# Two attentions whose maxima, sums and output fold leave float32 on TensorE

## The reference

```
x = x + cross_attention0(ctx, layernorm(x))   # 8 heads of 128, keys and values from [norm(x), norm(ctx)]: 2113 rows
x = x + experts0(layernorm(x))                # top 2 of 8 experts
x = x + cross_attention1(ctx, layernorm(x))   # 8 heads of 32, keys and values from ctx: 1601 rows
x = x + experts1(layernorm(x))                # top 2 of 8 experts
# each attention: softmax(q k^T * scale) v, per head; attention 0 has an output projection Wo
```

## Time and profile before

| | us |
|---|---|
| runs, median of 3 | 2718.49 (2716.02 to 2721.48) |
| the profiled execution | 2723.15 |
| its span, first to last instruction | 2721.6 |
| TensorE busy in the span | 2477.8 (91%) |
| DVE, ACT, POOL busy | 1865.4, 1675.5, 1636.6 |

### The profile page before, as it was taken

How to read it: one execution, slowest core, us unless ns; L and a number is a source line. 1 busy time by engine, 2 the same in 40 slices (tenths; PEclk the granted TensorE clock), 3 DMA queues, 4 the chain that set the end, 5 groups by cost and what they waited for, 6 DMA issues and landing times. The chain is left out here.

```text
span 2721.6 us, 46305 instructions
## 1 busy us (share of the span) xinstructions
PE 2477.8 (91%) x15187; PEld 1489.6 (55%) x15314; DVE 1865.4 (69%) x3467; ACT 1675.5 (62%) x2694; POOL 1636.6 (60%) x1442
## 2 busy tenths in 40 slices
PE   4999999999999999999999389867999999869997
PEld 2455555555555555555554268734555554447886
DVE  5678767787777786777676565347787888677443
ACT  3465665556655566555555375436787878758664
POOL 3467766677667676656567244416676769825443
PEclk9999999999999999999999589979999999969999
DMA  3000000000000000000000383231111101076223
GB/s 117 25 1 1 4 22 1 1 1 1 25 1 1 1 1 1 1 1 1 1 1 0 112 243 78 41 101 40 32 41 26 48 19 30 3 215 188 46 46 66
DMA packets 88377, 107.92 MB, mean 40 GB/s; under 512 B 16322, under 2 KB 77715, under 8 KB 88163
## 3 DMA queue, kind: packets, MB, share of 16 engines
q1 hardware_dynamic: 67140, 76.37, 9.3%
q0 software_dynamic: 19200, 24.97, 5.7%
q10 hardware_dynamic: 1856, 4.19, 0.4%
HBM read 68.75 MB, written 25.88 MB: 35 GB/s over the span
## 5 line engine op out<-in xcount | busy, mean ns | idle before, releaser
L396 POOL TENSOR_TENSOR a_acc<-a_acc,a_pf 128x512 f32<-128x512 f32 (+1 forms) x480 | 645.3, 1344 | 388.0 <-ACT a_pf L524 367.8
L1993 POOL TENSOR_TENSOR c_pl<-c_pf,c_ph 128x512 f16<-128x512 f32 x320 | 378.3, 1210 | 169.0 <-ACT c_ph L2092 168.7
L524 ACT ACTIVATE a_pf<-a_psS 128x1024 f32<-128x1024 f32 (+1 forms) x288 | 281.2, 976 | 303.8 <-PE a_psS L663 300.2
L813 DVE TENSOR_TENSOR a_pl<-a_pf,a_ph 128x512 f16<-128x512 f32 x448 | 405.4, 914 | 28.2 <-ACT a_ph L530 28.2
L789 DVE TENSOR_REDUCE a_mx<-a_psA 128x1 f32<-128x512 f32 x512 | 344.9, 685 | 48.8 <-PE a_psA L600 42.6
L530 ACT ACTIVATE a_ph<-a_psS 128x1024 f16<-128x1024 f32 (+1 forms) x288 | 281.0, 976 | 0.0
L1303 POOL DMA_INDIRECT f_sums<-f_xn,f_sidx x78 | 138.9, 1781 | 228.1 <-DVE f_xn L1668 191.6
L2324 DVE TENSOR_REDUCE c_mx<-c_psA 128x1 f32<-128x512 f32 x384 | 251.0, 685 | 34.4 <-PE c_psA L2163 32.4
L2085 ACT ACTIVATE c_pf<-c_psS 128x1024 f32<-128x1024 f32 x192 | 197.7, 1030 | 89.4 <-PE c_psS L2197 88.5
L784 DVE TENSOR_TENSOR a_vl<-a_psA,a_vh 128x256 f16<-128x256 f32 (+1 forms) x272 | 115.2, 423 | 167.2 <-ACT a_vh L469 164.3
L1162 DVE TENSOR_TENSOR f_xn<-f_xn 128x256 f16<-128x256 f32 x312 | 129.6, 424 | 127.8 <-ACT f_xn L1133 123.5
(11 more groups left out here) (329 smaller groups left out, 6382.8 us busy)
## 6 DMA issues: line engine op xcount, KB each, us to landing
f_stage<-in_L_ffn_w SPq DMA_DIRECT2D x16, 1024.0 KB, 5.6
f_stage<-in_L_ffn_W SPq DMA_DIRECT2D x16, 1024.0 KB, 5.3
c_kst<-c_khs SPq DMA_DIRECT2D x64, 100.1 KB, 2.2
a_cx<-in_ctx SPq DMA_DIRECT2D x4, 1536.0 KB
c_cx<-in_ctx SPq DMA_DIRECT2D x12, 512.0 KB, 4.1
f_xrow<-f_xn SPq DMA_DIRECT2D x8, 512.0 KB, 3.2
f_sums<-X SPq DMA_DIRECT2D x2, 2048.0 KB, 12.4
c_kst<-c_kls SPq DMA_DIRECT2D x32, 100.1 KB, 2.2
```

The source lines that it names most:

```text
L396: g.tensor_tensor(acc[0:k, p, :], acc[0:k, p, :], pf[0:k, q % RF, i, :], ALU.add).then_inc(s_acc, 1)
L524: act.activation(pf[0:r, q % RF, 0:k, :], psS[q % 2][0:r, 0:k, :], ACT.Exp, scale=SCALE).then_inc(s_pF, 1)
L813: v.tensor_tensor(pl[0:r, q % RP, i, :], pf[0:r, q % RF, i, :], ph[0:r, q % RP, i, :], ALU.subtract).then_inc(s_pL, 1)
L1993: g.tensor_tensor(pl[0:r, q % RP, i, :], pf[0:r, q % RF, i, :], ph[0:r, q % RP, i, :], ALU.subtract).then_inc(s_pG, 1)
```

## The change

In both attentions three operations of TensorE on float32 operands are replaced.

- Attention 0, maxima: X and ACT's copy go. POOL multiplies a diagonal of -1 (`minus`, bfloat16) with the maxima, broadcast, so that `mrow` holds each maximum negated on a diagonal; the unchanged fourth matmul with ones adds up the column. POOL does it in unit 7 behind its additions, and TensorE waits for it at the fourth matmul of the next head's first tile.
- Attention 0, sums: ACT makes a float16 high half of `acc` at the beginning of unit 1 of the next head, POOL the low half at the beginning of unit 2, and S takes both against a float16 column. To fit float16, the exponentials are lifted by a factor of 16 through a bias column, and the column of fours becomes 4/16, the output's scale 1/(64 x 16).
- Attention 1, maxima: `mc` and the identity are float16, X is a plain matmul.
- Attention 1, output: after `out_copy`, ACT makes the high half at the end of unit 4 and DVE the low half at the beginning of unit 5; both lie in the buffer of `pw`, whose next write now waits for F. F moves from unit 4 to unit 5, place 2, with twice the matmuls, in float16.

```diff
@@ attention0, head_items
-                               (6, 3, ("L", m)), (7, 2, ("X", m))):
+                               (6, 3, ("L", m))):
@@ gpsimd
+            def sum_lo(n):
+                g.wait_ge(s_sh, n + 1)
+                if n >= 1:
+                    g.wait_ge(s_it, IDX[("S", n - 1)] + 1)
+                g.tensor_tensor(sl[:, :], acc[:, n % 2, :], sh[:, :], ALU.subtract).then_inc(s_sl, 1)
+
+            def row(n):
+                g.wait_ge(s_mc, n + 1)
+                g.tensor_tensor(mrow[:, n % 2, :].rearrange("p (t q) -> p t q", q=P),
+                                minus[:, :].unsqueeze(1).broadcast_to([P, ST, P]),
+                                mc[:, n % 2, :].unsqueeze(2).broadcast_to([P, ST, P]), ALU.mult).then_inc(s_mrow, 1)
...
+            row(0)
...
+                    if n >= 1 and u == SUM_AT:
+                        sum_lo(n - 1)
                     sums(n, u)
+                    if u == TOP and n + 1 < NH:
+                        row(n + 1)
@@ scalar
-                elif what[0] == "X":
-                    act.wait_ge(s_it, i + 1)
-                    act.activation(mrow[0:1, what[1] % 2, :], ps[0:1, :], ACT.Copy, scale=-1.0).then_inc(s_ah, 1)
+            def sum_hi(n):
+                act.wait_ge(s_acc, added(uid(n, U - 1)))
+                if n >= 1:
+                    act.wait_ge(s_it, IDX[("S", n - 1)] + 1)
+                act.activation(sh[:, :], acc[:, n % 2, :], ACT.Copy).then_inc(s_sh, 1)
...
+                    if n >= 1 and u == SUM_AT - 1:
+                        sum_hi(n - 1)
...
                     act.activation(pf[0:r, q % RF, 0:k, :], psS[q % 2][0:r, 0:k, :], ACT.Exp,
-                                   scale=SCALE).then_inc(s_pF, 1)
+                                   bias=lift[0:r, 0:1], scale=SCALE).then_inc(s_pF, 1)
@@ tensor
-                    pe.wait_ge(s_acc, added(uid(n, U - 1)))
+                    pe.wait_ge(s_sl, n + 1)
                     for it in range(ST):
-                        ins = pe.matmul(ps[:, it:it + 1], acc[:, n % 2, it * P:(it + 1) * P], four[:, :], start=True,
-                                        stop=True)
+                        for part in (sh, sl):
+                            ins = pe.matmul(ps[:, it:it + 1], part[:, it * P:(it + 1) * P], quarter[:, :],
+                                            start=part is sh, stop=part is sl)
...
-                        pe.wait_ge(s_ah, after_act(("X", n)))
                 triple(ps, kh[:, p, js], kl[:, p, js], qh[:, p, :], ql[:, p, :], True, False)
+                if u == 0 and i == 0:
+                    pe.wait_ge(s_mrow, n + 1)
                 ins = pe.matmul(ps, oneb[:, 0:r], mrow[:, p, :], start=False, stop=True)
@@ attention1, head_items
-            at[LAG][2].append(("F", n - 1))
+            at[LAG + 1][2].append(("F", n - 1))
@@ scalar
+            def out_hi(n):
+                act.wait_ge(s_oF, n + 1)
+                if n >= 1:
+                    act.wait_ge(s_it, IDX[("F", n - 1)] + 1)
+                act.activation(ofh[:, :], of[:, :], ACT.Copy, scale=1.0 / 64).then_inc(s_oH, 1)
...
                     if u == WHOLE:
                         if n >= 1:
-                            act.wait_ge(s_pv, uid(n - 1, WHOLE) + 1)
+                            act.wait_ge(s_it, IDX[("F", n - 1)] + 1)
...
                     for what in places[2] + places[3]:
                         item(what)
+                    if n >= 1 and u == LAG:
+                        out_hi(n - 1)
@@ tensor
-                        ins = pe.transpose(ps[0:1, it * P:(it + 1) * P], mc[:, n % 2, it:it + 1], identf[:, :])
+                        ins = pe.matmul(ps[0:1, it * P:(it + 1) * P], mc[:, n % 2, it:it + 1], ident[:, :], start=True,
+                                        stop=True)
...
-                    pe.wait_ge(s_oF, n + 1)
+                    pe.wait_ge(s_oL, n + 1)
                     for it in range(ST):
-                        ins = pe.matmul(ps[:, it * (DH + 1):(it + 1) * (DH + 1)], of[:, it * P:(it + 1) * P],
-                                        fold[:, :], start=True, stop=True)
+                        for part in (ofh, ofl):
+                            ins = pe.matmul(ps[:, it * (DH + 1):(it + 1) * (DH + 1)], part[:, it * P:(it + 1) * P],
+                                            fold[:, :], start=part is ofh, stop=part is ofl)
@@ vector
+            def out_lo(n):
+                v.wait_ge(s_oH, n + 1)
+                v.scalar_tensor_tensor(ofl[:, :], of[:, :], 1.0 / 64, ofh[:, :], ALU.mult, ALU.subtract).then_inc(s_oL, 1)
...
+                    if n >= 1 and u == LAG + 1:
+                        out_lo(n - 1)
```

More of the change, by code:

```diff
@@ L12 @@
 import itertools
+import math
 from contextlib import ExitStack
@@ L150, in opening @@
         out.insert(out.index(("M", 0, 0, 0)), ("B", 0))
-        return out + [("L", 0), ("B", 1), ("V", 0, v), ("X", 0)]
+        return out + [("L", 0), ("B", 1), ("V", 0, v)]
     OPEN = opening()
@@ L261, in attention0 @@
         oneb = sb("oneb", [P, P], BF16)
+        minus = sb("minus", [P, P], BF16)
         onef = sb("onef", [P, P], F32)
-        four = sb("four", [P, 1], F32)
+        quarter = sb("quarter", [P, 1], F16)
+        lift = sb("lift", [P, 1], F32)
         zcol = sb("zcol", [P, 1], F32)
@@ L299, in attention0 @@
         s_mc = sem("mc")
+        s_mrow = sem("mrow")
         s_sP = sem("sP")
@@ L343, in _ @@
         def _(g):
-            for t, v in ((mhalf, -0.5), (onef, 1.0), (four, 4.0), (mv, 0.0), (oneb, 1.0), (mrow, 0.0), (zcol, 0.0)):
+            for t, v in ((mhalf, -0.5), (onef, 1.0), (quarter, 4.0 / LIFT), (lift, math.log(LIFT)), (mv, 0.0), (oneb, 1.0), (zcol, 0.0)):
                 g.memset(t[:], v).then_inc(s_const, 1)
-            g.wait_ge(s_const, 7)
+            g.tensor_scalar(minus[:, :], identf[:, :], -1.0, None, ALU.mult).then_inc(s_const, 1)
+            g.wait_ge(s_const, 8)
             pools = [0]
@@ L425, in _ @@
                             item(what)
+            sum_lo(NH - 1)
             for what in CLOSE:
@@ L501, in out_hi @@
                     act.wait_ge(s_it, IDX[("O", n - 1, 1)] + 1)
-                act.activation(oh[:, :], psO[:, :], ACT.Copy, scale=1.0 / 64).then_inc(s_oH, 1)
+                act.activation(oh[:, :], psO[:, :], ACT.Copy, scale=1.0 / (64 * LIFT)).then_inc(s_oH, 1)
             for what in OPEN:
@@ L530, in _ @@
                     act.activation(ph[0:r, q % RP, 0:k, :], psS[q % 2][0:r, 0:k, :], ACT.Exp,
-                                   scale=SCALE).then_inc(s_pH, 1)
+                                   bias=lift[0:r, 0:1], scale=SCALE).then_inc(s_pH, 1)
                     for what in places[2] + places[3]:
                         item(what)
+            sum_hi(NH - 1)
             out_hi(NH - 1)
@@ L610, in item @@
                     n = what[1]
-                    pe.wait_ge(s_acc, added(uid(n, U - 1)))
+                    pe.wait_ge(s_sl, n + 1)
                     for it in range(ST):
-                        ins = pe.matmul(ps[:, it:it + 1], acc[:, n % 2, it * P:(it + 1) * P], four[:, :], start=True,
-                                        stop=True)
-                elif what[0] == "X":
-                    n = what[1]
-                    pe.wait_ge(s_mc, n + 1)
-                    for it in range(ST):
-                        ins = pe.transpose(ps[0:1, it * P:(it + 1) * P], mc[:, n % 2, it:it + 1], identf[:, :])
+                        for part in (sh, sl):
+                            ins = pe.matmul(ps[:, it:it + 1], part[:, it * P:(it + 1) * P], quarter[:, :],
+                                            start=part is sh, stop=part is sl)
                 elif what == ("B", 0):
@@ L1911, in attention1 @@
         s_oF = sem("oF")
+        s_oH = sem("oH")
+        s_oL = sem("oL")
         s_rl = sem("rl")
@@ L1973, in rstds @@
                 g.tensor_scalar(ve[:, :], mv[:, :, 1], EPS, None, ALU.add).then_inc(s_pool, 1)
-                g.wait_ge(s_pool, b + 1 if b == 0 else 2 + b + 1)
+                g.wait_ge(s_pool, b + 1 if b == 0 else 3 + b + 1)
                 g.tensor_tensor(rstd[:, :], ve[:, :], mhalf[:, :], ALU.pow).then_inc(s_rstd, 1)
@@ L2095, in _ @@
                         item(what)
+                    if n >= 1 and u == LAG:
+                        out_hi(n - 1)
+            out_hi(NH - 1)
         @block.tensor
@@ L2381, in _ @@
             out_copy(NH - 1)
+            out_lo(NH - 1)
             for what in CLOSE:
```

31 lines of the change are left out of this document (19 added, 12 removed).

## The result

The changed kernel takes 2775.19 us (median of 4 runs, 2769.04 to 2777.64) against 2718.37 for the kernel before on the same chip: ratio 1.0202, interval 1.019 to 1.0214. It is slower by 2%, where I forecast no change, and lies above my range of 2696 to 2738. The profiled execution took 2773.67 us with a span of 2772.1, against 2723.15 and 2721.6.

A forecast was written before the change was run, and what follows sets the result against it. TensorE bounds attention 0 (99% busy); in attention 1 three other engines run close to the head's time. Attention 0's +13.1 and attention 1's -14.1 give -1.0 on 2723.15, less 4.66 for the median: 2717 us, range 2696 to 2738.

The forecast's parts named there:

- X removed: Attention 0: turning the maxima leaves TensorE, 0.43 us in each of 31 heads, -13.3 us.
- S in float16, and the lift: Attention 0: float16 sums save 0.57 us in each of 32 heads, -18.2; the exponentials' bias column costs +2.2.
- the row, late: Attention 0 head ends: TensorE waits for POOL's row behind unit 7's additions, +42.5 us, between 34 and 52.
- start and end: Attention 0: -0.5 us at the start, +0.4 at the end for the sums' halves.
- The rest has cover: Attention 0: the sums' halves on ACT (0.6 us) and POOL (1.15) cost nothing, POOL being idle 14.5 us a head.
- r: Duration of POOL's row instruction at attention 0's head ends: taken as 1.4 us, between 1.1 and 1.75.
- case 4: Attention 0: DVE's low half has the port first, the row takes 1.75 us at 28 boundaries, +8.8: 2727 us; chance 23%.
- Heads without preparation: Attention 1, 14 heads: DVE's chain replaces TensorE's 0.78 us saving, 0.2 kept each, -2.8; bounds -10.9 and +2.8.
- Case 5: Attention 1: `out_lo` meets POOL and takes 1.2 us instead of 0.7, +12 us: 2730; chance 16%.
- Heads with preparation: Attention 1, 18 heads: new chain covered, 0.78 us saved each, -14.0, of which 2 goes to small waits: -12.0.
- X in float16: Attention 1: four float16 matmuls turn the maxima in 0.22 us instead of 0.43, 0.21 saved a head.
- my signs for a wrong forecast: Row waits under 30 or over 55 us; row outside 1.0-1.8; sums not half a microsecond shorter; late attention-1 heads outside 13.3-14.1.

The follow-up runs named there:

- run 4: Kernel before, with only attention 0's sums in float16 halves and the lifted exponentials; maxima's row and attention 1 as before: 2717.39 us, ratio 0.9974.
- run 3: Changed kernel with POOL's row of maxima in unit 7 moved ahead of its two additions: 2722.20 us, ratio 1.0 against the kernel before.
- Run 2: Attention 1 as changed, attention 0 as in the kernel before: 2739.82 us, ratio 1.0068.
- Run 10: Attention 0 as before; attention 1 makes both output halves but leaves them unused, F staying float32 at its old place: 2748.98 us.
- run 6: Kernel before, with only attention 1's maxima and identity in float16 and four float16 matmuls for X: 2724.27 us, ratio 0.9999.
- run 7: Only attention 1 changed; in 14 heads without preparation `out_lo` reads one operand from PSUM, the output's low half left out: 2734.32 us, ratio 1.0038.
- run 8: Only attention 1 changed, with DVE making both output halves straight from PSUM and ACT's step gone: 2733.04 us, ratio 1.0035.

## Why the prediction was wrong

Attention 0, by the steps of the sum (measured: differences of the stage between before, run 4, run 3 and after, which add up to +35.6):

| step | predicted | measured |
|---|---|---|
| X removed | -13.3 | -13.8 |
| S in float16, and the lift | -18.2 + 2.2 | -6.3 |
| the row, late | +42.5 | +55.7 |
| start and end | -0.1 | within the above |
| attention 0 | +13.1 | +35.6 |

- **X: right**, to 0.01 us in 26 of 31 heads.
- **S: the saving right, its cover wrong.** 0.61 is saved against 0.57. "The rest has cover" is the step that failed: I showed that POOL was idle 14.5 us a head and concluded that its low half and ACT's high half were free. Idle time on average did not help: run 4 has six heads longer than before, with TensorE waiting for low halves of DVE and POOL. Some 12 us of 18.9 were given back, 2 of them expected.
- **The lift: 2.2 expected, at most 1 measured.** The size of the instruction was right (90 ns, where I had 75 to 80), its place was hidden. The 93 ns of the Trainium skill (ScalarE: Activation LUTs, "What ACT_TABLE_LOAD costs"), which I cited, is nearer to the 90.
- **The row: mechanism right, size wrong by 13 us.** Not r on average: 1.43, where I took 1.4. POOL's free time was wrong. I read it from the trace before and moved only TensorE by the removed X. But TensorE feeds ACT, and ACT feeds DVE's low halves, so these moved too, by a few tenths against POOL's second addition: enough to turn round who waits for whom at nine head ends, where that addition is 1.4 longer. That the removed X and ACT's removed copy are what moved them is argued from the two timelines; run 4 rules out the sums and the lift, but the late row itself was not separated. The boundary at which I had r - 0.76 (801.31 against 802.13) became 816.66 against a due time of 816.15 (0.22 behind the third matmul at 815.93): r + 0.6.

In the prediction's classes, the stalls came out so:

| head ends | predicted stall | measured |
|---|---|---|
| twelve of r + 0.1 | 1.5 | 0.9 to 1.6, 1.4 on average |
| nine of r - 0.76 | 0.64 | 2.05 at six, 0.64 at three |
| three of r + 1.45 | 2.85 | 3.65, though the row itself took 1.08 |
| three of r + 0.75 | 2.15 | 1.7 |
| three with nothing | 0 | 0.5 (the row took 2.5) |
| the last | 3.6 | 2.7 |
| all 31 | 42.5 | 51.3 |

So the long additions cost 8.5 at six head ends and 2.4 at three more, and other ends pay 2 of that back. To the 51.3 the half clock at three ends adds 5.9, which the prediction did not have, and at the end of the attention some 1.8 is hidden: 55.7 in all with small rests. I had priced the contention for the row alone (case 4, r = 1.75) and not for what stands ahead of it.

Attention 1: predicted -14.1, measured +16.6.

- **Heads without preparation: +0.2 kept predicted, 1.34 lost.** The failed step is "`out_lo`, like its two-input subtraction 0.68". I took the duration of the earlier trace rows that stands alone, with POOL 12.54 of 13.87 us busy beside it. Case 5 named this meeting but priced it at 1.2; it was 1.55, and the low halves behind it went from 730 to 1275 ns, which no case had. The six instructions behind `out_lo` were placed right, and took longer than I gave them: 18.6 in the 14 heads, against -2.8.
- **Heads with preparation: -12 predicted.** Run 2 has 14 of them at +3.9 together and three at -7.3. The three are the half-clock heads. In the others F's 0.57 is not gained and 0.28 a head is lost. Run 10, with the same added work and F at its old place, has twelve of these 14 within 0.02 of before and two 1.07 longer. So in the twelve `out_hi` and `out_lo` themselves are covered, and it is F, in its new form, place and wait, that gains nothing there.
- **X in float16: -0.21 a head predicted, -0.01 measured.** I put the matmul's length at 128 columns of a stream of 512-column ones; the group is 0.31 long, and a longer gap ahead of it eats most of the 0.13 that is saved (run 6).
- **The end, +0.7 predicted:** the last head length has +1.2 to +1.3, and is in the numbers above.

Of my signs for a wrong forecast the heads of attention 1 above 14.1 came, and POOL's row over 1.8, but at three head ends only. The listed waits for the row, 47.8, stayed within my 30 to 55: a total inside its bounds did not show that its parts were wrong.

What stays open: which single meeting causes each of the six longer heads of run 4, and by which of its two added steps; and why the low halves of DVE in attention 1 lengthen even where `out_lo` has one SBUF input (run 7). Both fit the exclusion of POOL and DVE; neither was isolated. Nor is it shown why the half clock comes in some heads and not in others with the same wait (run 8).

## What to carry to other kernels

- Work moved off TensorE goes into a queue: ask what stands ahead of it there, and whether the instruction that TensorE waits for can go first. The same row, put in X's place, was worth -13.8 us ahead of two additions and +41.9 behind them.
- When TensorE is made earlier, replay the engines that it feeds before you read another engine's free time from the old trace: a two-input instruction that stood beside nothing may now stand beside its rival.
- DVE, 84% busy with in-order work next to POOL at 90%, had no cover for a 0.7 us instruction. Price it at the contended duration, and its followers too. The fold saved 0.6 us of TensorE and two instructions paid for it; here it was better left in float32.

## What the runs showed of the hardware that was not expected

- Eight float16 matmuls with 128x128 weights and one moving column started 0.025 us apart.
- Four float16 matmuls with one weight column and 128 moving ones started 0.055 apart (float32: 0.11), but the first stood 0.31 behind a 512-column matmul where the float32 one stood 0.21 behind it, and the next matmul came 0.15 behind the fourth (float32: 0.11). From the matmul ahead to the successor it was 0.62 instead of 0.65 (run 6).
- A TensorE wait of 3.5 us inside attention 0 was followed by 3 to 7 us at the 1.2 GHz level, three times of three; there the listed waits of up to 1.9, and the last one of 2.57, were followed by none. The length of the wait does not settle it: in run 8 a listed wait of 1.54 in attention 1 was followed by some 3 us at that level in two heads and by none in the ones beside them.
- A DVE instruction took 1.55 us with two SBUF inputs beside POOL's subtractions and 0.69 with one of them from PSUM (run 7), and a POOL addition went from 1.27 to 2.7 beside DVE's low halves. Each direction occurs.
